# One loop per expert in the expert MLP, with tile numbers and the GELU table loaded once ahead of the loops

## The chip, the cores and the metric

The kernel runs on one core of a Trainium2 chip. The metric is the device time of one execution in microseconds (us). The kernel before takes 2174.18 us, the median of 3 runs (2167.58 to 2176.35).

## The reference, cut to what matters

The program is a graph block of two layers on 1250 nodes of 512 features. The change touches only the mixture of experts in the first layer: each token goes to 2 of 8 experts, and each expert is a two-layer MLP (512 to 2048 to 512 features) with an exact GELU. D is 512, E is 8 and K is 2.

```python
def _L0_ffn_ref(x, ln_g, ln_b, w_r, b_r, W1, b1, W2, b2):
    ...
    h = (x - mu) * jax.lax.rsqrt(var + LN_EPS) * ln_g + ln_b
    logits = jnp.einsum('btd,ed->bte', h, w_r) + b_r
    topk_vals, topk_idx = jax.lax.top_k(logits, K)
    gates = jax.nn.softmax(topk_vals, axis=-1)
    hf = h.reshape(B * T, d)
    hid = jax.nn.gelu(jnp.einsum('nd,edf->nef', hf, W1) + b1, approximate=False)
    expert_stack = jnp.einsum('nef,efd->ned', hid, W2) + b2
    ...
    return x + mixed
```

## The kernel before, in words

Every engine has its own program, written by hand; they meet at semaphores. Around 860 to 1500 us of the span stands the expert stage. Tokens have been sorted by expert into `tokens_sorted` and padded so that each tile of 128 rows belongs to one expert. `first_tile_int` holds nine whole numbers: `first_tile_int[e]` is the number of the first tile of expert e, and the last is the count of tiles. They come out of the data, so every engine reads them into registers to know where its loops end (`expert_bounds`, L719, one `value_load` per number, which is a TENSOR_LOAD at L721 and some register instructions).

On each of PE, ACT and DVE the stage is an outer loop of four rounds `i`, and in a round two inner loops over tiles `t`: `a = 0` for expert 2i, `a = 1` for expert 2i + 1 (even and odd expert below). Each engine reads three bounds at the start of a round. The weights lie in two sets of buffers, chosen by `a`: W1 and half of W2 in `big_a` or `big_b`, the other half in `wide`. SP loads them (L910 to L919): expert e + 2 as soon as the last tile of expert e is through.

A tile goes through 16 chunks `f` of 128 hidden units (`FC` = 16). PE multiplies W1's chunk with the transposed tile `tile_T` into one of four banks (L2571). ACT applies GELU with the expert's bias twice, into `hid` and rounded into `hid_hi` (L1370), and copies W2's chunk rounded into `w2_hi` (L1346). DVE takes the remainders, `hid_lo` (L1902) and `w2_lo` (L1909). Two chunks behind, PE multiplies three products of hidden and W2 parts into the bank of the result (L2561, L2562, L2563). Behind the last up-projection PE transposes the next tile's rows (L2541), and ACT and DVE each write half of `tile_T` (L1352, L1895); `down(14)` and `down(15)` follow on PE. DVE copies the result to `tile_out` (L1942). POOL has its own loop over all tiles, without experts: it loads the rows of the tile after next (L1117) when PE has transposed, and stores `tile_out` (L1120).

The text of ACT's inner loops does not load the table of GELU; the builder puts an ACT_TABLE_LOAD ahead of an activation wherever the table in place may be another. Before the stage it is the one of the square root (L1340). Whoever builds the first inner loop's body can't tell which table it finds, so that body holds two such loads.

Of the kernel before, what the change touches and what calls it, by code (L numbers as in the profile page):

```python
# [6 lines left out]
P = 128  # L7
# [37 lines left out]
def graph_block_kernel(nc, A, out):  # L45
# [5 lines left out]
    C = D // P  # L51
# [34 lines left out]
    with ctx:  # L86
# [1061 lines left out]
        def _(act):  # L1148
# [207 lines left out]
            act.wait_ge(tiles_ready, 1)  # L1356
            act.sem_inc(gelu_done, UP_BANKS)
            tile_T_half(1)
            with act.Fori(0, EX // 2) as i:
                bounds = expert_bounds(act, i)  # L1360
                for a in range(2):
                    lo, hi = bounds[a:a + 2]
                    with act.Fori(lo, hi) as t:
                        act.wait_ge(ew2_loaded[a], i * 32 + 32)
                        w2_leading(t, a, 0)
                        for f in range(FC):
                            act.wait_ge(up_done, t * FC + f + 1)
                            act.wait_ge(chunk_used, t * FC + f + 1)
                            for dst in (hid, hid_hi):
                                last = nc.scalar.activation(dst[:, f % HID_SLOTS, :], psum[:, f % UP_BANKS, 0:P], ACT.Gelu,  # L1370
                                                            bias=expert_bias_T[:, bass.ds(i * (2 * FC) + a * FC + f, 1)])
                            last.then_inc(gelu_done, 1)

                            if f + 1 < FC - 1:
                                w2_leading(t, a, f + 1)
                            if f == FC - 1:
                                w2_leading(t, a, f)
                        tile_T_half(t + 2)
# [171 lines left out]
        def _(dve):  # L1550
# [375 lines left out]
            dve.sem_inc(tile_out_ready, 1)  # L1926
            tile_transposed_out(1)
            dve.sem_inc(tile_out_free, 1)
            with dve.Fori(0, EX // 2) as i:
                bounds = expert_bounds(dve, i)  # L1930
                for a in range(2):
                    with dve.Fori(bounds[a], bounds[a + 1]) as t:
                        w2_rest(t, a, 0)
                        for f in range(FC):
                            hidden_rest(t, f)
                            if f + 1 < FC - 1:
                                w2_rest(t, a, f + 1)
                        w2_rest(t, a, FC - 1)
                        tile_transposed_out(t + 2)
                        dve.wait_ge(chunk_used, t * FC + FC + HID_SLOTS)  # L1940
                        dve.wait_ge(tile_out_free, t + 1)
                        nc.vector.tensor_copy(tile_out, psum[:, Y_BANK, :]).then_inc(tile_out_ready, 1)  # L1942
# [234 lines left out]
        def _(pe):  # L2177
# [357 lines left out]

            for b in range(8):
                pe.wait_ge(bank_free[b], before_experts[b])
# [9 lines left out]
            with pe.Fori(0, EX // 2) as i:  # L2547
                bounds = expert_bounds(pe, i)
                for a in range(2):
                    lo, hi = bounds[a:a + 2]  # L2550
                    pe.wait_ge(ew1_loaded[a], i * 32 + 32)
                    pe.sem_inc(loop_entered, 1)
                    with pe.Fori(lo, hi) as t:
                        def down(f):
                            if f == 0:
                                pe.wait_ge(tile_out_ready, t + 1)
# [227 lines left out]
```

## Time and profile before

| | us |
|---|---|
| median of 3 runs (lowest to highest) | 2174.18 (2167.58 to 2176.35) |
| the profiled execution's own time | 2170.96 |
| its span, from first to last instruction | 2169.3 |
| PE matmuls busy | 2046.8 (94%) |
| DVE busy | 1310.9 (60%) |
| ACT busy | 1056.2 (49%) |
| POOL busy | 527.6 (24%) |
| granted TensorE clock, mean | 0.974 of full speed |

A busy share is that of the whole span, of which the expert stage is some 630 us. "PE" are the matmuls, "PEld" the weight loads that overlap them; names ending in "q" are an engine's sequencer, whose register, branch and load instructions do not count as busy. "Issue" is idle time in which an engine waited for nothing that the profile shows. The granted clock of 1.0 is TensorE at 2.4 GHz, 0.5 at 1.2 GHz.

### The profile page before, as it was taken

How to read it: one execution, taken by the hardware profiler on the slowest of the kernel's cores; microseconds unless marked ns; L12 is line 12 of the kernel's file. 1: busy time of each engine (PE TensorE's matmuls, PEld its weight loads, DVE VectorE, ACT ScalarE, POOL GpSimd, SP SyncE). 2: the span in 40 equal slices, each digit the busy share in tenths (PEclk: the TensorE clock that was granted, in tenths of full speed). 3: DMA queues.
4: the chain of work that ended last, by engine and by line, in shares of the span. 5: the costliest groups of instructions: out<-in, count | busy, mean ns of one | idle time of the engine just before them, and what ended most of it. 6: DMA issues, size and time to landing. Idle time of an engine off the chain costs nothing.

```text
span 2169.3 us, 42548 instructions
## 1 busy us (share of the span) xinstructions
PE 2046.8 (94%) x13564; PEld 1485.4 (68%) x13565; DVE 1310.9 (60%) x2651; ACT 1056.2 (49%) x2327; POOL 527.6 (24%) x567
## 2 busy tenths in 40 slices
PE   7899899999999988999999999996899999999998
PEld 4544344444444466888888888885697888778886
DVE  3311699999999977555555555655613445644444
ACT  6531244444444422776777777774243322554443
POOL 3100477777766752100000000004000000400000
PEclk9999999999999997999999999998999999999999
DMA  6651588888888875548104400044500200310000
GB/s 217 227 175 45 157 238 238 239 237 236 238 238 238 237 302 189 207 174 298 51 19 174 174 19 19 19 174 158 194 11 10 88 20 20 112 44 10 10 10 19
DMA packets 141915, 297.44 MB, mean 137 GB/s; under 512 B 28925, under 2 KB 70662, under 8 KB 137239
## 3 DMA queue, kind: packets, MB, share of 16 engines
q1 hardware_dynamic: 96933, 159.09, 21.2%
q0 software_dynamic: 36592, 130.56, 19.9%
q10 hardware_dynamic: 8322, 6.89, 1.0%
q8 instruction: 43, 0.70, 0.1%
q14 instruction: 25, 0.20, 0.0%
HBM read 242.31 MB, written 54.17 MB: 137 GB/s over the span
## 4 chain that ended last, share of the span: by engine, by line
PE 86%; DVE 4%; issue 3%; ACT 3%; DMA 2%; POOL 1%; ACTq 0%; POOLq 0%; DVEq 0%; PEldq 0%
PE psum L2571 14%; PE psum L2425 11%; PE psum L2387 9%; PE psum L2710 7%; PE psum L2743 5%; PE psum L2616 4%; PE psum L2561 4%; PE psum L2562 4%; PE psum L2563 3%; PE psum L2607 3%; PE psum L2647 3%; PE psum L2413 3%; PE psum L2637 3%; PE psum L2286 2%; PE psum L2661 1%
## 5 line engine op out<-in xcount | busy, mean ns | idle before, releaser
L1068 POOL DMA_INDIRECT big_b<-sender_table,wide x360 | 376.8, 1047 | 209.4 <-issue 118.6
L2425 PEld LDWEIGHTS psum<-big_b,wide 128*32 128x32 f32 x3600 | 165.4, 109 | 193.5 <-issue 130.3
L2571 PEld LDWEIGHTS psum<-xn_T,big_b 128*128 128x128 f32 x2048 | 261.9, 191 | 21.2 <-issue 3.1
L1250 ACT ACTIVATE wide<-wide 128x290 bf16<-128x290 f32 x360 | 168.5, 527 | 219.8 <-PE psum L2425 161.9
L2425 PE MATMUL psum<-big_b,wide 128*32 128x256 f32 (+2 forms) x3600 | 270.0, 387 | 0.0
L2571 PE MATMUL psum<-xn_T,big_b 128*128 128x128 f32 x2048 | 265.0, 275 | 0.0
L2387 PE MATMUL psum<-w_mlp,wide 64*128 64x512 f32 x728 | 206.2, 643 | 5.3 <-DVE big_b L1733 3.6
L1909 DVE TENSOR_TENSOR w_lo<-wide,w_hi 128x512 fp32r<-128x512 f32 x184 | 127.3, 692 | 117.9 <-ACT w_hi L1346 117.9
L2561 PE MATMUL psum<-w_hi,hid_hi 128*128 128x512 f32 x368 | 176.1, 478 | 10.1 <-DVE w_lo L1909 7.2
L1733 DVE TENSOR_TENSOR big_b<-big_b,psum 128x768 f32<-128x768 f32 x180 | 169.4, 941 | 0.0
L1732 DVE TENSOR_TENSOR big_b<-big_b,psum 128x768 f32<-128x768 f32 x180 | 168.7, 937 | 0.0
L2710 PE MATMUL psum<-xn_T,wide 128*128 128x256 f32 (+1 forms) x640 | 154.7, 388 | 2.9 <-ACT shid_hi L1542 2.9
L1346 ACT ACTIVATE w_hi<-wide 128x512 fp32r<-128x512 f32 x184 | 115.8, 629 | 70.7 <-PE psum L2563 70.7
L2562 PE MATMUL psum<-w_hi,hid_lo 128*128 128x512 f32 x368 | 146.1, 397 | 0.0
L2563 PE MATMUL psum<-w_lo,hid_hi 128*128 128x512 f32 x368 | 144.3, 392 | 0.0
L1370 ACT ACTIVATE xn_T<-psum,table 128x128 f32<-128x128 f32 x368 | 130.6, 355 | 25.4 <-PE psum L2571 25.3
L1117 POOL DMA_DIRECT2D xn_T<-tokens_sorted x23 | 12.5, 542 | 527.3 <-PE psum L2541 527.3
L2710 PEld LDWEIGHTS psum<-xn_T,wide 128*128 128x128 f32 (+1 forms) x640 | 123.9, 195 | 23.4 <-issue 3.9
L2571 PEld LDWEIGHTS psum<-xn_T,big_a 128*128 128x128 f32 x896 | 121.9, 202 | 20.5 <-issue 12.6
L1370 ACT ACTIVATE hid_hi<-psum,table 128x128 fp32r<-128x128 f32 x368 | 133.7, 363 | 0.0
L2571 PE MATMUL psum<-xn_T,big_a 128*128 128x128 f32 x896 | 123.8, 287 | 10.3 <-issue 10.3
L1909 DVE TENSOR_TENSOR w_lo<-big_b,w_hi 128x512 fp32r<-128x512 f32 x128 | 88.4, 691 | 74.6 <-ACT w_hi L1346 74.6
(457 smaller groups left out, 3680.9 us busy)
## 6 DMA issues: line engine op xcount, KB each, us to landing
big_a<-in_L_ffn_W SPq DMA_DIRECT2D x12, 2048.0 KB, 13.8
big_b<-in_L_ffn_W SPq DMA_DIRECT2D x12, 2048.0 KB, 13.4
wide<-in_L_ffn_W SPq DMA_DIRECT2D x8, 2048.0 KB, 23.5
wide<-edge_hidden SPq DMA_DIRECT2D x91, 128.0 KB
edge_hidden<-wide SPq DMA_DIRECT2D x21, 512.0 KB, 3.0
tokens_sorted<-zeros SPq DMA_DIRECT2D x29, 256.0 KB, 3.4
adj_dram<-big_a SPq DMA_DIRECT2D x1, 6400.0 KB, 23.3
xn_T<-tokens_sorted POOLq DMA_DIRECT2D x25, 256.0 KB, 2.9
```

Of the source, the lines that this page charges most:

```text
L1068: nc.gpsimd.indirect_dma_start(out=sent[q][:, j, :], out_offset=None, in_=sender_table, in_offset=bass.IndirectOffsetOnAxis(ap=record[k][q ...
L1370: last = nc.scalar.activation(dst[:, f % HID_SLOTS, :], psum[:, f % UP_BANKS, 0:P], ACT.Gelu, bias=expert_bias_T[:, bass.ds(i * (2 * FC) + ...
L1732: nc.vector.tensor_tensor(prod[q][:, :, 5:8, :], s1, w[:, :, 2:3, :].to_broadcast([P, 2, 3, MUL]), ALU.mult)
L1733: nc.vector.tensor_tensor(prod[q][:, :, 2:5, :], s1, w[:, :, 3:4, :].to_broadcast([P, 2, 3, MUL]), ALU.mult)\
L1909: nc.vector.tensor_tensor(w2_lo[:, f % 2, :], w2, w2_hi[:, f % 2, :].bitcast(F32), ALU.subtract).then_inc(w2_split, 1)
L2387: last = nc.tensor.matmul(tile_w[q % 2][:, j, :], h3_slot[q][halves[j], :], w_mlp4[halves[j], :], start=True, stop=True)
L2425: return nc.tensor.matmul(msg_psum[k].rearrange("p (c u) -> p c u", u=MUL)[bands[g], cols, :], hot_y[q][:, j, y, :], p[:, of, :], start=Fa ...
L2561: nc.tensor.matmul(psum[:, Y_BANK, :], hid_hi[:, h, :], w2_hi[:, w, :], start=(f == 0), stop=False)
L2562: nc.tensor.matmul(psum[:, Y_BANK, :], hid_lo[:, h, :], w2_hi[:, w, :], start=False, stop=False)
L2563: nc.tensor.matmul(psum[:, Y_BANK, :], hid_hi[:, h, :], w2_lo[:, w, :], start=False, stop=(f == FC - 1))\
L2571: last = nc.tensor.matmul(psum[:, f % UP_BANKS, 0:P], ew1[a][:, c, f * P:f * P + P], tile_T[:, c, :], start=(c == 0), stop=(c == C - 1))
L2710: last = nc.tensor.matmul(out_b[0:r, 0:n], sw1_cols[:, c, j * P:j * P + r], xn_T[:, c, n0:n0 + n], start=(c == 0), stop=(c == C - 1))
```

## The change

The outer loop over pairs is unrolled: on PE, ACT and DVE there are now eight loops over tiles, one per expert. The bounds of all experts are read once, ahead of them (eight reads per engine; expert 0 starts at 0), at a place where `tiles_ready` says that they are there. ACT loads the GELU table once, by hand, behind its reads and ahead of the first `tile_T` half. The wait for W2's weights stands once per expert ahead of ACT's loop. The bias of a chunk is addressed by a constant. PE no longer reads the count of tiles behind the loops. SP and POOL are unchanged.

```diff
-        def expert_bounds(eng, i):
-
-            return [eng.value_load(first_tile_int[0:1, bass.ds(2 * i + k, 1)], min_val=min(k, 1), max_val=TILES - (k < 2))
-                    for k in range(3)]
+        def expert_bounds(eng):
+
+            return [0] + [eng.value_load(first_tile_int[0:1, e:e + 1], min_val=e, max_val=TILES - (EX - e)) for e in range(1, EX + 1)]
...
             act.wait_ge(tiles_ready, 1)
+            bounds = expert_bounds(act)
+            nc.scalar.preload_act_table(ACT.Gelu)
             act.sem_inc(gelu_done, UP_BANKS)
             tile_T_half(1)
-            with act.Fori(0, EX // 2) as i:
-                bounds = expert_bounds(act, i)
-                for a in range(2):
-                    lo, hi = bounds[a:a + 2]
-                    with act.Fori(lo, hi) as t:
-                        act.wait_ge(ew2_loaded[a], i * 32 + 32)
-                        w2_leading(t, a, 0)
...
-                                                            bias=expert_bias_T[:, bass.ds(i * (2 * FC) + a * FC + f, 1)])
...
+            for e in range(EX):
+                a = e % 2
+                act.wait_ge(ew2_loaded[a], e // 2 * 32 + 32)
+                with act.Fori(bounds[e], bounds[e + 1]) as t:
+                    w2_leading(t, a, 0)
...
+                                                        bias=expert_bias_T[:, e * FC + f:e * FC + f + 1])
...
             dve.sem_inc(tile_out_ready, 1)
+            dve.wait_ge(tiles_ready, 1)
+            bounds = expert_bounds(dve)
             tile_transposed_out(1)
             dve.sem_inc(tile_out_free, 1)
-            with dve.Fori(0, EX // 2) as i:
-                bounds = expert_bounds(dve, i)
-                for a in range(2):
-                    with dve.Fori(bounds[a], bounds[a + 1]) as t:
...
+            for e in range(EX):
+                a = e % 2
+                with dve.Fori(bounds[e], bounds[e + 1]) as t:
...
             transposes(("biasT",), [bias_rows[:, :]])
 
+            pe.wait_ge(tiles_ready, 1)
+            bounds = expert_bounds(pe)
             for b in range(8):
                 pe.wait_ge(bank_free[b], before_experts[b])
 
...
             pe.wait_ge(tile_loaded, 16)
             tile_transposes()
             pe.sem_inc(chunk_used, HID_SLOTS)
-            with pe.Fori(0, EX // 2) as i:
-                bounds = expert_bounds(pe, i)
-                for a in range(2):
-                    lo, hi = bounds[a:a + 2]
-                    pe.wait_ge(ew1_loaded[a], i * 32 + 32)
-                    pe.sem_inc(loop_entered, 1)
-                    with pe.Fori(lo, hi) as t:
...
-            count = pe.value_load(first_tile_int[0:1, EX:EX + 1], min_val=EX, max_val=TILES)
-            pe.wait_ge(tile_out_ready, count + 1)
-            pe.wait_ge(tile_T_ready, count + 1)
-            pe.wait_ge(tile_T_half_ready, count + 1)
+            for e in range(EX):
+                a = e % 2
+                pe.wait_ge(ew1_loaded[a], e // 2 * 32 + 32)
+                with pe.Fori(bounds[e], bounds[e + 1]) as t:
...
+            pe.wait_ge(tile_out_ready, bounds[EX] + 1)
+            pe.wait_ge(tile_T_ready, bounds[EX] + 1)
+            pe.wait_ge(tile_T_half_ready, bounds[EX] + 1)
```

How the instructions stand, at two places. First ACT, where it enters the stage and the first even expert's loop. Before (L1352 is the first `tile_T` half, L1346 the copy of W2's chunk into `w2_hi`, L1370 the GELU; "table" in a TENSOR_LOAD is the buffer that holds the tile numbers):

```order
L1352 ACTIVATE xn_T<-psum,table 128x128 x2
L1359 UNCONDITIONAL_BRANCH
L1359 ISA
L721 TENSOR_LOAD table
L721 ISA x3
...
L1363 UNCONDITIONAL_BRANCH
L1363 ISA
L1345 ISA
L1346 ACT_TABLE_LOAD
L1346 ACTIVATE w_hi<-big_a 128x512
...
L1370 ACT_TABLE_LOAD
L1370 ACTIVATE xn_T<-psum,table 128x128
```

And of the change (the line numbers are one less):

```order
L721 TENSOR_LOAD table
L721 ISA x2
...
L1357 ACT_TABLE_LOAD
L1351 ACTIVATE xn_T<-psum,table 128x128 x2
L1363 UNCONDITIONAL_BRANCH
L1363 ISA
L1345 ACTIVATE w_hi<-big_a 128x512
L1366 REGISTER_ALU
L1369 ACTIVATE xn_T<-psum,table 128x128
L1369 ACTIVATE hid_hi<-psum,table 128x128
```

The reads, eight now, and one table load have moved ahead of the first `tile_T` half; the two table loads inside the loop are gone, and the register instruction ahead of each GELU pair with them. The next ACT_TABLE_LOAD stands behind the last expert's loop (L1300).

Second PE, where the stage begins and at the end of a round. Before (L2541 are the four transposes, L2553 is the loop over tiles, L2547 the one over pairs):

```order
L2541 MATMUL psum<-ident,xn_T 128x128 x4
L2547 UNCONDITIONAL_BRANCH
L2547 ISA
L721 TENSOR_LOAD table
L721 ISA x3
...
L2571 MATMUL psum<-xn_T,big_a 128x128 x4
...
L2553 COMPARE_AND_BRANCH
L2547 REGISTER_ALU
L2547 COMPARE_AND_BRANCH
L2580 TENSOR_LOAD table
```

And of the change, at the start of the stage and from the loop of one expert to that of the next (L2543 are the transposes, L2552 is the loop over tiles):

```order
L721 TENSOR_LOAD table
L721 ISA x2
L2543 MATMUL psum<-ident,xn_T 128x128 x4
L2552 UNCONDITIONAL_BRANCH
...
L2552 COMPARE_AND_BRANCH
L2552 UNCONDITIONAL_BRANCH
L2552 ISA
L2568 ISA
L2570 MATMUL psum<-xn_T,big_b 128x128 x4
```

The reads stand ahead of the wait for the first tile, not between the transposes and the first up-projection, and between two experts there are only the end of one loop and the start of the next.

## Rows read from the trace of the kernel before

**Rows 1.** The page, chain that ended last: shares of the span by line.

```profile
PE psum L2571 14%; PE psum L2425 11%; PE psum L2387 9%; PE psum L2710 7%; PE psum L2743 5%; PE psum L2616 4%; PE psum L2561 4%; PE psum L2562 4%; PE psum L2563 3%; PE psum L2607 3%; PE psum L2647 3%; PE psum L2413 3%; PE psum L2637 3%; PE psum L2286 2%; PE psum L2661 1%
```

**Rows 2.** Timeline of POOL: start, length (us), engine, line, operation.

```profile
897.10 0.56 POOL L1117 DMA_DIRECT2D xn_T<-tokens_sorted  x1 [18.17 <-PE psum L2541]
...
1496.76 0.61 POOL L1117 DMA_DIRECT2D xn_T<-tokens_sorted  x1 [5.27 <-PE psum L2541]
```

**Rows 3.** Stretches between L1117's issues: engines' busy us (count), PEclk, DMA share, GB/s.

```profile
897.10:924.54 27.44, 26.42 (x180) 23.64 (x180) 15.79 (x36) 21.54 (x53) 1.11 (x3) 1.00 0.22 83
951.00:977.43 26.43, 26.12 (x180) 23.57 (x180) 15.71 (x36) 18.87 (x51) 1.08 (x3) 1.00 0.06 21
977.43:1009.49 32.06, 29.09 (x180) 26.23 (x180) 15.80 (x36) 21.54 (x53) 1.08 (x3) 0.89 0.75 278
1141.69:1171.93 30.24, 26.61 (x180) 23.64 (x180) 15.79 (x36) 21.54 (x53) 1.08 (x2) 1.00 0.79 295
...
1410.83:1442.89 32.06, 29.14 (x180) 26.29 (x180) 15.81 (x36) 21.55 (x53) 1.09 (x3) 0.89 0.75 278
```

**Rows 4.** The same of PE, from a tile's first up-projection to L1117's issue.

```profile
1010.51:1035.95 25.44, 25.36 (x178) 1.00 0.95 350
1145.49:1171.93 26.44, 25.64 (x177) 1.00 0.82 321
...
981.28:1009.49 28.21, 28.12 (x177) 0.90 0.78 301
869.08:897.10 28.02, 27.90 (x177) 0.91 0.81 308
```

**Rows 5.** ACT's table loads in the stage: busy us, mean ns | idle before.

```profile
L1346 ACT ACT_TABLE_LOAD x7 | 9.0, 1283 | 6.9 <-issue 6.8
L1370 ACT ACT_TABLE_LOAD x7 | 9.0, 1283 | 6.3 <-PE psum L2571 6.1
```

**Rows 6.** Timeline at expert 4's entry; in brackets idle time before, and releaser.

```profile
1145.49 2.94 PE L2571 MATMUL psum<-xn_T,big_a 128*128 128x128 f32 x24 [2.61 <-issue]
...
1146.75 1.28 ACT L1370 ACT_TABLE_LOAD   x1 [1.35 <-PE psum L2571]
...
1149.14 0.47 PE L2561 MATMUL psum<-w_hi,hid_hi 128*128 128x512 f32 x1 [0.72 <-DVE hid_lo L1902]
```

**Rows 7.** Line 721 at that entry, by sequencer: ns min/median/max, first and last start.

```profile
L721 ACTq TENSOR_LOAD <-table x3: 273/275/281, 1141.5 to 1142.7; - x3
...
L721 PEldq TENSOR_LOAD <-table x3: 298/301/307, 1142.6 to 1144.2; - x3
...
L721 DVEq TENSOR_LOAD <-table x3: 300/300/314, 1143.7 to 1145.1; - x3
```

**Rows 8.** Waits of the expert stage: us in total, times, longest.

```profile
ACT w_hi L1346 <- PE psum L2563: 137.9, 299, 1.3
```

**Rows 9.** Timeline of PE at the start of the stage.

```profile
865.57 1.08 PE L2541 MATMUL psum<-ident,xn_T 128*128 128x128 f32 x4 [7.59 <-DMA xn_T<-tokens_sorted]
869.08 5.45 PE L2571 MATMUL psum<-xn_T,big_a 128*128 128x128 f32 x24 [2.42 <-issue]
```

**Rows 10.** Timelines of DVE and of ACT at the same place.

```profile
866.69 0.73 DVE L1895 TENSOR_SCALAR xn_T<-psum,table 128x128 f32<-128x128 f32 x2 [7.25 <-PE psum L2541]
...
866.69 0.81 ACT L1352 ACTIVATE xn_T<-psum,table 128x128 f32<-128x128 f32 x2 [8.49 <-PE psum L2541]
```

**Rows 11.** Expert 3's last weights: issue in SP's timeline, and line 919's landing.

```profile
980.41 10.18 SPq L919 DMA_DIRECT2D wide<-in_L_ffn_W  x1
...
DMA to landing us min/median/max: 23.9/23.9/23.9
```

**Rows 12.** Timeline of DVE in the first tile of expert 3.

```profile
1011.41 0.68 DVE L1909 TENSOR_TENSOR w_lo<-big_b,w_hi 128x512 fp32r<-128x512 f32 x1
```

**Rows 13.** DMA queues between 850 and 1120 us: packets, MB, share.

```profile
q8 instruction: 4, 0.07, 0.1%
```

More of the change, by code:

```diff
@@ L1926, in _ @@
             dve.sem_inc(tile_out_ready, 1)
+            dve.wait_ge(tiles_ready, 1)
+            bounds = expert_bounds(dve)
             tile_transposed_out(1)
             dve.sem_inc(tile_out_free, 1)
[L1929 to L1942 removed]
+            for e in range(EX):
+                a = e % 2
+                with dve.Fori(bounds[e], bounds[e + 1]) as t:
+                    w2_rest(t, a, 0)
+                    for f in range(FC):
+                        hidden_rest(t, f)
+                        if f + 1 < FC - 1:
+                            w2_rest(t, a, f + 1)
+                    w2_rest(t, a, FC - 1)
+                    tile_transposed_out(t + 2)
+                    dve.wait_ge(chunk_used, t * FC + FC + HID_SLOTS)
+                    dve.wait_ge(tile_out_free, t + 1)
+                    nc.vector.tensor_copy(tile_out, psum[:, Y_BANK, :]).then_inc(tile_out_ready, 1)
             for t in range(NT + 1):
@@ L2580, in _, with down @@
-            count = pe.value_load(first_tile_int[0:1, EX:EX + 1], min_val=EX, max_val=TILES)
-            pe.wait_ge(tile_out_ready, count + 1)
-            pe.wait_ge(tile_T_ready, count + 1)
-            pe.wait_ge(tile_T_half_ready, count + 1)
+            for e in range(EX):
+                a = e % 2
+                pe.wait_ge(ew1_loaded[a], e // 2 * 32 + 32)
+                with pe.Fori(bounds[e], bounds[e + 1]) as t:
+                    def down(f):
+                        if f == 0:
+                            pe.wait_ge(tile_out_ready, t + 1)
+                        pe.wait_ge(w2_split, t * FC + f + 1)
+                        pe.wait_ge(hid_split, t * FC + f + 1)
+                        h, w = f % HID_SLOTS, f % 2
+                        nc.tensor.matmul(psum[:, Y_BANK, :], hid_hi[:, h, :], w2_hi[:, w, :], start=(f == 0), stop=False)
+                        nc.tensor.matmul(psum[:, Y_BANK, :], hid_lo[:, h, :], w2_hi[:, w, :], start=False, stop=False)
+                        nc.tensor.matmul(psum[:, Y_BANK, :], hid_hi[:, h, :], w2_lo[:, w, :], start=False, stop=(f == FC - 1))\
+                            .then_inc(chunk_used, 1)
+                    pe.wait_ge(tile_T_ready, t + 1)
+                    pe.wait_ge(tile_T_half_ready, t + 1)
+                    for f in range(FC):
+                        pe.wait_ge(gelu_done, t * FC + f + 1)
+                        for c in range(C):
+                            last = nc.tensor.matmul(psum[:, f % UP_BANKS, 0:P], ew1[a][:, c, f * P:f * P + P], tile_T[:, c, :],
+                                                    start=(c == 0), stop=(c == C - 1))
+                        last.then_inc(up_done, 1)
+                        if f >= 2:
+                            down(f - 2)
+                    pe.wait_ge(tile_loaded, t * 16 + 32)
+                    tile_transposes()
+                    down(FC - 2)
+                    down(FC - 1)
```

46 lines of the change are left out of this document (11 added, 35 removed).

## The prediction

> **What bounds the kernel now.** I read the page first: its chain of waits gives the expert stage's matmuls (L2571, L2561 to L2563) 25% of the span [rows 1]. Such a share does not say what an edit of that stage is worth, so I went to the stage itself. POOL reloads `tile_rows` once per tile (L1117), always behind the same four transposes on PE, so its issues are a clock with one tick per tile. There are 23 ticks, the first at 897.10 us and the last at 1496.76 [rows 2]: 599.66 us for 22 periods, 27.26 us each. The table of stretches between two ticks [rows 3] shows that they are not alike. A tile of an odd expert takes 26.43 us, the second tile of expert 0 takes 27.44, and the first tile of experts 2, 4 and 6, behind the turn of the pair loop, takes 32.06, 30.24 and 32.06. From the ticks, experts 0 to 7 have 2, 2, 1, 5, 2, 8, 2 and 1 tiles. PE is 26.12 us busy in the 26.43 of a plain tile, and ACT waits for PE in nearly every chunk (137.9 us over 299 waits, 0.46 us each [rows 8]). So PE bounds a plain tile, and what only relieves ACT or a sequencer inside it can't show; what can move is the excess over some 26.44 us.
>
> **What makes up the excess.** The next table measures from the first up-projection of a tile to the next tick [rows 4]: 25.44 us in an odd tile; 26.44 in the first tile of expert 4, at full clock; 28.21 in that of expert 2, where the granted clock averages 0.90 (part of the stretch stands at the lower level, 1.2 GHz); 28.02 at 0.91 in the first tile of all. So at full clock the body of an even tile costs 1.00 us more than an odd one. The order of instructions names what the even body has and the odd one has not: two ACT_TABLE_LOADs per tile, in seven tiles, 1283 ns each [rows 5]. That is 2.57 us of ACT, of which 1.00 reaches PE: the rest lies beside PE's 24 up-projection matmuls, which run ahead of the first GELU. The timeline of expert 4's entry [rows 6] shows both parts: PE waits 2.61 us ("issue") before the up-projection at 1145.49, and 0.72 us more at 1149.14 for hid_lo, which is late behind the second table load at 1146.75. In the first of these gaps the sequencers make three TENSOR_LOADs each, of 0.30 us and with register work behind them, so that on PE their starts lie 0.8 us apart, on DVE 0.7 and on ACT 0.6 [rows 7].
>
> **The change, part by part.**
> - *Table loads out of the even tiles.* All eight loops now hold Copy, Gelu and Identity alone, and one load stands ahead of them. Six even tiles at 1.00: **6.0 us** (the seventh, the stage's first tile, is counted below).
> - *Tile numbers no longer read at a pair's start.* Of expert 4's 30.24 us, 26.44 are a plain tile and 1.00 the tables, so its entry is 2.80; three entries: **8.4 us**. What an entry costs afterwards is what the step from an even to an odd expert costs now: expert 1's first period runs from 924.54 to 951.00, 26.46 [rows 3], 0.02 over a plain one. At 0.04 for each of seven entries, **0.3 us** is given back.
> - *Clock.* Experts 2 and 6 take 1.82 us longer than expert 4 with the same work, at a granted clock of 0.89 against 1.00 [rows 3], and the lower level comes after PE's 2.6 us pause. Without the pause I take the dip as gone: **3.6 us**. Ends: 0, if both dips stay, and 3.6.
> - *First tile.* PE starts its last four transposes at 865.57 and the up-projection only at 869.08 [rows 9], since all three engines first enter the pair loop and read its bounds. Now only `tile_T` is needed; ACT's half of it takes 0.81 us from 866.69 [rows 10], so the start can be near 867.7, 1.4 us earlier. But PE stands at the lower level here (24 matmuls in 5.45 us, against 2.94 at full clock [rows 6]), and time won at half speed is worth half if the clock rises when it did. Ends 0.7 and 1.4; I take **1.0**. The tables cost nothing in this tile, since 28.02 less 25.44 is 2.58 and the slow matmuls alone account for 2.51 of it.
> - *Eight reads ahead of the stage, per engine.* By the spacing above, 6.4 us on PE, 5.6 on DVE, 4.8 on ACT. Their cover is the wait for the first tile's rows: PE is idle for 7.59 us up to 865.57 [rows 9], DVE for 7.25 and ACT for 8.49 up to 866.69 [rows 10]. ACT has the table load, 1.28, on top. All is hidden, by 1.2 us at the least. If a read cost a third of a whole entry, 0.93, eight would be 7.5: PE just in time, DVE 0.2 late, ACT (8.7 in all) 0.3 late. I take 0, with 0.3 as the other end.
> - *Register work off ACT.* The bias address needs no register any more, and ACT waits on `ew2_loaded` once per expert, not per tile: 0, because ACT waits for PE in the chunks [rows 8]. PE's read behind the loops goes too: 0, as PE waits there for the first z rows anyway.
> - *Which transfer comes next?* Only expert 3's weights have a single tile (expert 2's) to arrive in. Their last part is issued at 980.41 and lands 23.9 us later, at 1004.3 [rows 11], 26.9 us after the tick at 977.43. Now expert 2's tile ends 26.44 after it, and ACT wants that weight at once: some 0.4 us late. But DVE takes its remainder only at 1011.41 [rows 12], 1.92 behind the tick at 1009.49, and the copy before it takes 0.6, so up to about 1.3 us is swallowed. 0, with 1 us as the bad end.
>
> **Sum.** 6.0 + 8.4 - 0.3 + 3.6 + 1.0 = 18.7 us. From the other side: 22 periods of 26.44 are 581.7, against 599.66 now; the 17.9 between them answer to the 17.7 of the terms without the first tile. The profiled execution took 2170.96 us, so it would become 2152.3. It lies 3.2 us below the median of the runs shown, 2174.18 (2167.58 to 2176.35); against that median, on which I forecast, it is **2155.5 us**.
>
> **A rule weighed.** Entries by the outer loop's back branch idle PE 2.61 us [rows 6], and the very first entry, which no back branch precedes, 2.42 [rows 9]: the jump back over two bodies costs 0.2 us at most, and a back branch over one body or the first run through expert 1's code costs nothing that the period shows (26.43 and 26.46) [rows 3]. "Runtime: NRT & Kernel Launch" of the Trainium skill, section Instruction fetch mechanics, says that a taken branch stalls for a fetch when its target is outside a small window of recent pages. By it the back branch could be most of the 8.4 us, which leaves the sum as it is; but it also speaks against this change, which makes four times the loop code. What that would do here is rival 2.
>
> **The rivals.**
> 1. *The gap stays.* If PE's pause is loop set-up and not the reads, every even entry keeps it and only the tables and the first tile's end go: 6.0 + 1.0 = 7.0 us, 2167.2. For it: the view says "issue". Against: three reads at 0.8 fill 2.4 of the 2.6 us, and odd experts enter the same kind of loop without a gap. 5%.
> 2. *The code of eight bodies does not stay at hand* (slower). A tile's body is 180 matmuls and 180 weight loads on PE, with waits between [rows 3], and the instruction queue brought in only 4 pieces between 850 and 1120 us [rows 13]: once through experts 0 and 1, then looped. If now the branch back inside each expert had to fetch its body anew, each of 15 such branches (23 tiles, 8 experts) could cost as much as the entry gap, 2.61 us: 39.2 us, less 18.7, or 2194.7. The point from which it decides is 18.7 / 15 = 1.25 us per branch. Against it: one body is half of the pair that stayed at hand, and each loop is as long as before. 4%.
> 3. *The clock keeps its dips*, due by time and not to the pause. For it: expert 4's entry has the pause and no dip. Against: two of three pauses have one, and long stretches without a pause have none. 18.7 - 3.6 = 15.1, 2159.1. 13%.
> 4. *The loads stay where they were.* In the changed order no table load stands in the loops and no TENSOR_LOAD between them, so this is 1%, at 2174.
>
> **Numbers.** Forecast 77%; rivals 5, 4, 13 and 1%. About 0.5%, 10.9 us, is what a measurement of this kernel can tell from no change. The range takes the sum's ends (a gain of 14.8 to 19.1), rival 3, and a median that may fall some 4 us to either side as the runs shown do: 2147 to 2164; rivals 1, 2 and 4 stay outside. Faster: forecast and rival 3 less 2% for their slow edge, 0.88. Same: that edge and rivals 1 and 4, 0.08. Slower: rival 2, 0.04.
>
> **What would show it.** One ACT_TABLE_LOAD at L1357 near 863 us and none in the tiles; ticks of POOL's reload 26.4 apart from first to last, so some 582 us in all; PE's "issue" idle before the up-projection under 1 us per entry; eight TENSOR_LOADs per engine, done before 866; a granted clock of 1.00 from the second tile to the last. It is wrong if ticks within an expert grow, if the first tick comes later than 897, or if what the stage saves returns behind it, in the wait for the z rows.

## The result, and the profile after

The changed kernel takes 2155.49 us (median of 6 runs, 2150.12 to 2160.32), the kernel before 2171.59 in 6 runs beside it (2167.58 to 2176.35). The ratio is 0.9918, with a 95% interval of 0.9902 to 0.9934: faster by 0.8%. The profiled execution took 2152.54 us, 18.4 less than the 2170.96 of before; the prediction's sum was 18.7. By the medians the gain is 16.1.

| | before | after |
|---|---|---|
| profiled execution / its span, us | 2170.96 / 2169.3 | 2152.54 / 2151.0 |
| PE, DVE busy, us | 2046.8, 1310.9 | 2038.7, 1311.0 |
| ACT, POOL busy, us | 1056.2, 527.6 | 1037.8, 545.9 |
| first and last tick of POOL's reload | 897.10, 1496.76 | 896.10, 1477.66 |
| 22 periods | 599.66 | 581.56 |
| last tick to the end of the span | 672.5 | 673.3 |

So 18.1 us came from the 22 periods, the first tick stands 1.0 earlier, and 0.8 went again behind the stage: 18.3 of span. The ticks, in POOL's timeline of the changed kernel (start, length, line; they answer to [rows 2]):

```profile
896.10 0.56 POOL L1116 DMA_DIRECT2D xn_T<-tokens_sorted  x1 [17.42 <-PE psum L2543]
...
1477.66 0.61 POOL L1116 DMA_DIRECT2D xn_T<-tokens_sorted  x1 [5.28 <-PE psum L2543]
```

The stretches between ticks, of the changed kernel (length, then busy us of PE, PEld, DVE, ACT and POOL with counts, granted clock, DMA share, GB/s). In order: second tile of expert 0, expert 1's first, experts 2's and 4's first, and the stage's last but one. They answer to [rows 3]:

```profile
896.10:922.53 26.43, 26.13 (x180) 23.58 (x180) 15.71 (x36) 18.84 (x51) 1.11 (x2) 1.00 0.26 96
922.53:948.94 26.41, 26.12 (x180) 23.58 (x180) 15.69 (x36) 18.81 (x51) 1.09 (x2) 1.00 0.90 338
975.38:1001.81 26.43, 26.12 (x180) 23.58 (x180) 15.71 (x36) 18.82 (x51) 1.08 (x2) 1.00 0.90 338
1133.98:1160.42 26.44, 26.12 (x180) 23.58 (x180) 15.72 (x36) 18.84 (x51) 1.08 (x3) 1.00 0.90 338
1424.78:1451.22 26.44, 26.12 (x180) 23.57 (x180) 15.72 (x36) 18.83 (x51) 1.09 (x3) 1.00 0.06 20
```

Every one of the 22 periods lies between 26.41 and 26.47. The 27.44 of the even tile is gone (ACT has 51 instructions there instead of 53 and 2.7 us less busy time), and so are the 32.06, 30.24 and 32.06 of the entries. PE is busy 26.12 of 26.44 in all of them; the clock is 1.00 throughout. At expert 4's entry, where before stood 2.61 of issue [rows 6], PE's timeline now shows only the wait that every tile has:

```profile
1134.21 0.50 PE L2560 MATMUL psum<-w_hi,hid_hi 128*128 128x512 f32 x1 [0.32 <-DVE w_lo L1908]
1134.55 0.40 PE L2561 MATMUL psum<-w_hi,hid_lo 128*128 128x512 f32 x1
1134.78 0.39 PE L2562 MATMUL psum<-w_lo,hid_hi 128*128 128x512 f32 x1
1135.01 2.74 PE L2570 MATMUL psum<-xn_T,big_a 128*128 128x128 f32 x23
```

The waits of the 22 periods (total, times, longest) say what bounds a tile now. PE waits for one thing alone, the last w_lo of a tile, 0.3 us each time:

```profile
...
DVE w_lo L1908 <- ACT w_hi L1345: 217.9, 331, 1.1
ACT w_hi L1345 <- PE psum L2562: 134.7, 286, 0.8
...
PE psum L2560 <- DVE w_lo L1908: 6.9, 22, 0.3
```

The start of the stage is the one place that does not look as forecast. PE's timeline there (it answers to [rows 9]):

```profile
860.69 0.24 PE L2446 MATMUL psum<-ident,src_int 24*128 24x24 f32 x1
865.17 1.09 PE L2543 MATMUL psum<-ident,xn_T 128*128 128x128 f32 x4 [4.24 <-DMA xn_T<-tokens_sorted]
```

ACT's timeline at the same place, against [rows 10], and then line 721 by sequencer (ns min/median/max, first and last start):

```profile
860.97 0.19 ACT L1341 ACTIVATE table<-psum 128x24 f32<-128x24 f32 x1 [15.49 <-PE psum L2446]
866.02 1.28 ACT L1357 ACT_TABLE_LOAD   x1 [4.86 <-issue]
867.31 0.81 ACT L1351 ACTIVATE xn_T<-psum,table 128x128 f32<-128x128 f32 x2
```

```profile
L721 PEldq TENSOR_LOAD <-table x8: 296/335/563, 855.0 to 860.1; - x8
...
L721 ACTq TENSOR_LOAD <-table x8: 273/280/553, 861.0 to 864.9; - x8
L721 DVEq TENSOR_LOAD <-table x8: 297/314/582, 861.1 to 865.7; - x8
```

The transposes end at 866.26, but ACT is not through with its eight reads and the table load before 867.30, so its half of tile_T starts 1.0 us late, and PE's first up-projection behind a wait of 2.10 for it. ACT began its reads late because PE's work ahead of L2446 ended late: the same 20 matmuls of L2532 took 14.19 us before, at a granted clock of 0.62, and take 17.43 now, at 0.50, which is the lower level of 1.2 GHz. PE's timelines, before and after:

```profile
843.75 14.19 PE L2532 MATMUL psum<-w_mlp,xn_T 8*128 8x512 f32 x20
```

```profile
843.47 17.43 PE L2532 MATMUL psum<-w_mlp,xn_T 8*128 8x512 f32 x20
```

### The profile page after: what moved, and what is told of

It reads as the page before. It is cut to its first block, busy times and chain, and to the rows that moved or that the text cites. A ratio compares the mean times of both kernels' runs of the same rounds, so it can differ in the third digit from the quotient of the medians.

```text
span 2151.0 us, 42029 instructions
## 1 busy us (share of the span) xinstructions
PE 2038.7 (95%) x13564; PEld 1480.0 (69%) x13565; DVE 1311.0 (61%) x2651; ACT 1037.8 (48%) x2314; POOL 545.9 (25%) x567
## 4 chain that ended last, share of the span: by engine, by line
PE 87%; DVE 4%; ACT 3%; issue 2%; DMA 2%; POOL 1%; ACTq 0%; POOLq 0%; DVEq 0%; PEldq 0%
PE psum L2570 14%; PE psum L2425 12%; PE psum L2387 9%; PE psum L2708 7%; PE psum L2741 5%; PE psum L2614 4%; PE psum L2560 4%; PE psum L2561 4%; PE psum L2562 3%; PE psum L2605 3%; PE psum L2413 3%; PE psum L2645 3%; PE psum L2635 3%; PE psum L2286 2%; PE psum L2659 1%
## 5 line engine op out<-in xcount | busy, mean ns | idle before, releaser
L1067 POOL DMA_INDIRECT big_b<-sender_table,wide x360 | 395.3, 1098 | 191.1 <-issue 79.4
L1730 DVE TENSOR_TENSOR big_b<-psum,big_b 128x512 f32<-128x512 f32 x180 | 121.2, 673 | 9.6 <-DMA big_b<-sender_table,wide 9.5
L2570 PEld LDWEIGHTS psum<-xn_T,big_a 128*128 128x128 f32 x896 | 116.9, 195 | 11.5 <-issue 3.6
```

Source lines behind the costliest of these rows:

```text
L1067: nc.gpsimd.indirect_dma_start(out=sent[q][:, j, :], out_offset=None, in_=sender_table, in_offset=bass.IndirectOffsetOnAxis(ap=record[k][q ...
L2570: last = nc.tensor.matmul(psum[:, f % UP_BANKS, 0:P], ew1[a][:, c, f * P:f * P + P], tile_T[:, c, :], start=(c == 0), stop=(c == C - 1))
```

## The experiments

Kernels of one group ran on one chip, beside the kernel before. The two kernels with added table loads in the first group, and all in the second, the kernel before among them, have one run each. In the first two groups the kernel before took 2243.15 and 2251.33 us; the work ahead of the stage is some 70 us longer there (first tick at 968.55 in the first run below, 897.10 in [rows 2]). Why is not known; the first and the third group bear the same chip number, so the chip does not explain it. So I read the stage by its ticks; the periods of plain tiles are the same there, 26.43 to 26.48. A period is named by the tile that it ends in.

### Which part of the gain is whose (first group)

**Table load alone ahead of the pair loop**, in the kernel before:

```diff
+            nc.scalar.preload_act_table(ACT.Gelu)
             act.sem_inc(gelu_done, UP_BANKS)
             tile_T_half(1)
```

> The kernel before, with one GELU table load by hand ahead of the first tile_T half; the pair loop and its reads stay, and the 14 table loads in the tiles vanish. My theory (a pair of loads in an even tile costs PE 1.00 us, the rest is covered): the second tiles of experts 0, 4 and 6 fall from 27.4 to 26.44 us, the first tiles of experts 2, 4 and 6 from 32.06, 30.24 and 32.06 to about 31.06, 29.24 and 31.06; first to last reload of tile_rows from 599.66 to about 593.7 us; the kernel 6 us faster. Rival (every load counts in full, 2.57 us a tile): second tiles 24.9 us or the stage some 15 us shorter. Rival (the loads carry the entry's gap too): entries fall to 26.44.

Measured: 2236.42 us, ratio 0.9971 (0.9956 to 0.9986). The stretches of expert 0's second tile, and of the entries of experts 2, 4 and 6:

```profile
968.55:995.02 26.47, 26.17 (x180) 23.56 (x180) 15.70 (x36) 18.86 (x51) 1.11 (x2) 1.00 0.12 41
1047.92:1078.89 30.97, 27.99 (x180) 25.20 (x180) 15.90 (x36) 19.09 (x51) 1.09 (x3) 0.94 0.77 288
1211.10:1240.39 29.29, 26.36 (x180) 23.57 (x180) 15.81 (x36) 18.99 (x51) 1.08 (x3) 1.00 0.81 304
1478.33:1509.24 30.91, 28.00 (x180) 25.20 (x180) 15.89 (x36) 19.09 (x51) 1.08 (x2) 0.94 0.77 288
```

Expert 0's second tile fell from 27.44 to 26.47, and experts 4's and 6's likewise (26.43, 26.44): 1.0 us per even tile, as the first term has it. One call ahead of the loops is enough; the builder puts no load into the loops then. Expert 4's entry keeps 29.29 less 26.44, 2.85 us, with PE's 2.61 of issue; two of three entries keep their dip, 1.6 to 1.7 us.

**The reads back at a pair's start, everything else as changed.** Eight loops stay, one table load stays ahead, and each engine reads three bounds by constant address ahead of each even expert's loop:

```diff
+                if a == 0:
+                    bounds = pair_bounds(pe, e)
-                with pe.Fori(bounds[e], bounds[e + 1]) as t:
+                with pe.Fori(bounds[a], bounds[a + 1]) as t:
```

> The changed kernel, with three tile numbers read on PE, ACT and DVE at the start of every even expert's loop, where the pair loop read them, and none ahead of the stage. Eight loops and the one table load stay. My theory (the entry's gap is the reads): first tiles of experts 2, 4 and 6 take about 29.2 us at full clock, or 31.0 where the granted clock falls after the pause; the stage from first to last reload 581.6 + 8.4 = 590.0, plus 1.8 for each dip; the kernel 8 to 14 us slower than the changed one. Rival (the gap is the pair loop's own branch or set-up): these tiles stay at 26.4 to 26.7 us and the time does not move.

Measured: 2230.42 us, ratio 0.9944 (0.9923 to 0.9964). The entries of experts 2, 4 and 6, and PE at expert 4's:

```profile
1053.73:1082.00 28.27, 26.37 (x180) 23.57 (x180) 15.80 (x36) 18.94 (x51) 1.08 (x2) 1.00 0.84 317
1214.18:1242.49 28.31, 26.36 (x180) 23.57 (x180) 15.80 (x36) 18.96 (x51) 1.08 (x3) 1.00 0.85 316
1480.40:1508.70 28.30, 26.37 (x180) 23.57 (x180) 15.80 (x36) 18.94 (x51) 1.08 (x2) 1.00 0.84 316
```

```profile
1217.00 1.27 PE L2580 MATMUL psum<-xn_T,big_a 128*128 128x128 f32 x9 [1.63 <-issue]
```

An entry costs 1.87 us over 26.43, not the 2.80 that the kernel before paid. The reads by constant address start 0.65 us apart on PE:

```profile
L725 PEldq TENSOR_LOAD <-table x3: 296/298/302, 1214.7 to 1216.0; - x3
```

Before it was 0.80 [rows 7], and there one more register instruction stood behind each. So of the 2.85 of an entry at full clock, two thirds are three reads as such; the other 0.98 is the address worked out from `i` and the turn of the outer loop, which this run does not tell apart. An estimate from the spacings: 0.15 more for each of three reads is 0.45, and some 0.5 is left for the turn of the loop. None of the three entries has a dip.

**Where a table load hides.** With the eight loops as changed, one more load per tile at the loop's start, and then loads on either side of the first copy:

```diff
                 with act.Fori(bounds[e], bounds[e + 1]) as t:
+                    if True:
+                        nc.scalar.preload_act_table(ACT.Gelu)
                     w2_leading(t, a, 0)
```

> The changed kernel, with one more GELU table load at the start of each of the 23 tiles, ahead of the copy of W2's first chunk. My theory (ACT waits 1.48 us for the first up-projection there, which covers 1.28): a tile stays at 26.44 us, the stage at 581.6. Rival (a load goes on the path in full, 1.28 each): 27.7 a tile, the stage 28 us longer.

> The changed kernel, with three more GELU table loads in each of the 23 tiles: one ahead of the copy of W2's first chunk and two behind it, ahead of the first GELU. My theory (a fixed cover of about 1.9 us at a tile's start, from 1.48 us of ACT's wait and some 0.4 us until hid_lo of chunk 0 is late for PE): 3.85 - 1.9 = 1.9 to 2.0 us a tile, so 28.4 us a tile and the stage about 43 us longer. Rival (no cover, 3.85 a tile): 30.3 a tile, 85 us longer. Rival (chunks catch up, since ACT has slack in each chunk): 26.44.

Measured with one: 2220.06 us, and no tile is longer, though ACT is 1.4 us busier:

```profile
1201.85:1228.28 26.43, 26.12 (x180) 23.57 (x180) 15.78 (x36) 20.23 (x52) 1.08 (x2) 1.00 0.91 338
```

In the second kernel the builder dropped one of the two loads that stood in a row, so it has two per tile, not three (x22 each in ACT's groups, 1283 ns), and it measures what two cost: 27.27 to 27.29 in every tile but the last, +0.84 for 2.57 us of ACT. PE waits once more than in a plain tile, at the first down-projection; the rest of the 0.84 is its busy time, 26.36 against 26.12 for the same matmuls:

```profile
1218.91:1246.20 27.29, 26.36 (x180) 23.65 (x180) 15.80 (x36) 21.52 (x53) 1.08 (x2) 1.00 0.86 328
```

```profile
1223.41 0.47 PE L2564 MATMUL psum<-w_hi,hid_hi 128*128 128x512 f32 x1 [0.61 <-DVE hid_lo L1905]
```

The cover is thus between 1.28 and 2.57, and 1.73 if all that passes it counts in full. Two loads cost 0.84 here and 1.00 in the even tiles of before. They stand at other places: before, the second one began only behind the wait for the up-projection [rows 6], here it stands ahead of that wait. That this is the 0.16 between them is not shown; that the 1.00 belongs to the loads is shown by the run with the table load alone. The last tile took 36.66 here, and 29.36 in the run with the table load alone; see the end of this section.

### Whose reads cost, and when the clock falls (second group)

**Reads back on PE alone, on ACT and DVE alone, and six reads instead of three on all.** The edits are that of the reads above, on the engines named; for six, `for n in (e, e + 1, e + 2, e, e + 1, e + 2)`.

> The changed kernel with the three reads at the start of each even expert on PE alone; ACT and DVE keep theirs ahead of the stage. With all three engines reading there, an entry takes 28.3 us, 1.87 more than a plain tile. My theory (PE's own reads are the gap, 1.63 us of them idle, since the other engines' start earlier or have cover): 28.1 to 28.3 us for the first tiles of experts 2, 4 and 6. Rival (DVE, last to read, sets the end): about 26.6 to 27.0. Rival (reads of the engines add up): near 27.1.

> The changed kernel with the three reads at the start of each even expert on ACT and DVE, and PE's ahead of the stage. My theory (ACT's copy of W2's first chunk comes 1.0 us late, which its wait covers; DVE's reads end some 1.2 to 1.4 us behind where w_lo of chunk 0 would start, which PE feels by 0 to 0.6 us): 26.4 to 27.1 us for the first tiles of experts 2, 4 and 6. Rival (DVE sets the end): 28.3.

> reads_back with every number read twice: six reads per engine at the start of an even expert. My theory (0.65 us per read with a constant address, on PE's path): an entry of 28.3 + 1.95 = 30.2 us at full clock. For the clock: if it falls because PE stood still long enough (it did in two of three pauses of 2.6 us and in none of 1.6 us), it falls behind at least two of these pauses of 3.6 us, and those entries take about 32. Rival (the dips were due to something else in the pair loop): 1.00 throughout and 30.2 for all three.

| reads at an even entry | time | entries 2, 4, 6 | over 26.44 | PE's issue idle | dips |
|---|---|---|---|---|---|
| three on all | 2230.42 | 28.27, 28.31, 28.30 | 1.85 | 1.63 | 0 of 3 |
| three on PE | 2239.72 | 28.44, 28.29, 28.31 | 1.9 | 1.62 | 0 of 3 |
| three on ACT and DVE | 2233.38 | 27.37, 27.36, 27.36 | 0.92 | none; 0.69 for hid_lo | 0 of 3 |
| six on all | 2248.52 | 31.87, 31.84, 31.87 | 5.4 | 3.54 | 3 of 3 |

The first row is the kernel of the first group. PE's own reads set the entry; the same reads on ACT and DVE come to rest behind them when all three read, and alone they still cost half, as hid_lo comes late. The last row's stretch, with the clock at 0.95, and PE at expert 4's entry:

```profile
1220.11:1251.95 31.84, 27.99 (x180) 25.20 (x180) 15.89 (x36) 19.09 (x51) 1.08 (x3) 0.95 0.75 281
```

```profile
1224.83 1.65 PE L2580 MATMUL psum<-xn_T,big_a 128*128 128x128 f32 x8 [3.54 <-issue]
```

PE's busy time tells the dip apart from the pause: 27.99 against 26.36 for the same 180 matmuls, 1.63 us. So three more reads added 1.9 of pause and 1.6 of clock. Over all runs, pauses of 1.6 us brought no dip (0 of 6), of 2.6 us two in three (the same two in the kernel before and in the one with the table load alone), of 3.5 us three in three. The dips belong to the pauses; why expert 4's entry escapes at 2.6 us is not shown.

**Three table loads per tile, kept apart** so that the builder drops none:

```diff
+                    nc.scalar.preload_act_table(ACT.Gelu)
                     w2_leading(t, a, 0)
+                    nc.scalar.preload_act_table(ACT.Gelu)
...
                         last.then_inc(gelu_done, 1)
+                        if f == 0:
+                            nc.scalar.preload_act_table(ACT.Gelu)
```

> The changed kernel with three table loads per tile and an activation between each, so that the builder keeps all three (of the two in a row in three_loads_all it kept one, and that run had two per tile: 27.28 us, 0.84 over a plain tile for 2.57 of loads, a cover of 1.73): ahead of W2's first copy, behind it, and behind the first chunk's GELU pair. My theory (one cover for the start of a tile, 1.73 us, and what passes it goes to PE in full): 3.85 - 1.73 = 2.1 us over, 28.5 to 28.6 us per tile. Rival (ACT's slack of 0.44 us in each chunk takes up a load placed behind the first chunk): 27.3 to 27.7.

Measured: 2268.21 us, 28.23 per tile, +1.79 for 3.85 us of ACT where 2.1 was expected. The third load, behind the first GELU, is late at the second down-projection and costs 0.95 of its 1.28:

```profile
1233.35 0.47 PE L2564 MATMUL psum<-w_hi,hid_hi 128*128 128x512 f32 x1 [0.61 <-DVE hid_lo L1905]
1235.89 0.47 PE L2564 MATMUL psum<-w_hi,hid_hi 128*128 128x512 f32 x1 [0.72 <-DVE hid_lo L1905]
```

The cover at a tile's start is used up by the first two, and only 0.33 of the third is taken up elsewhere.

### Can the start and the tile's end be had too? (third group)

Beside 11 runs of the kernel before (2171.84 us, 2168.36 to 2177.25), the changed kernel again, one with ACT's reads and table load ahead of its copy of the biases (a copy that waits for PE), and one with two more edits at a tile's end. There DVE wrote its half of tile_T ahead of the last w_lo, and PE waited for w_lo only ahead of the third product:

```diff
             nc.scalar.activation(dinv[:, :], full[:, 0:NT], ACT.Sqrt).then_inc(free, 1)
+            nc.scalar.preload_act_table(ACT.Gelu)
+            act.wait_ge(tiles_ready, 1)
+            bounds = expert_bounds(act)
             full, free = filled(act, ("biasT",))
...
-            act.wait_ge(tiles_ready, 1)
-            bounds = expert_bounds(act)
-            nc.scalar.preload_act_table(ACT.Gelu)
             act.sem_inc(gelu_done, UP_BANKS)
```

```diff
-                        pe.wait_ge(w2_split, t * FC + f + 1)
+                        pe.wait_ge(w2_hi_ready, t * FC + f + 1)
...
+                        pe.wait_ge(w2_split, t * FC + f + 1)
                         nc.tensor.matmul(psum[:, Y_BANK, :], hid_hi[:, h, :], w2_lo[:, w, :], start=False, stop=(f == FC - 1))\
```

> The changed kernel itself, beside the next two on the same chip. 22 tile periods of 26.44 us, 581.6 from first to last reload of tile_rows; against the kernel before a ratio near 0.992, or 0.9917 if the 18 us of the stage are all of it.

> The changed kernel with ACT's table load and its eight reads moved further ahead, before the wait for biasT's transpose, where ACT is idle. My theory (ACT's reads and the load end 0.9 us behind the first transposes now and hold up the first half of tile_T): the time from the first transposes on PE to the first reload of tile_rows falls from 30.9 us to 30.1 to 30.5, all other periods stay; the whole 0.4 to 0.9 us, too little to be seen in the time. Rival (DVE's reads end as late as ACT's and bind next): 30.9 again.

> early, and in each tile two more edits: PE waits for w2_lo only ahead of the third product of a chunk (for w2_hi ahead of the first), and DVE writes its half of the next tile_T ahead of the last chunk's w2_lo. My theory (a plain tile is 16 chunks of 1.587 us = 25.39 and 1.05 at its end, of which PE waits 0.3 for w2_lo and the next up-projection another 0.2 behind tile_T): 26.15 to 26.25 us per tile, the stage near 576, the kernel about 5 us faster than early. Rival (the end of a tile is bound by the chain over ACT's and DVE's tile_T halves alone, so PE's earlier matmuls only wait elsewhere): 26.44.

| | time (lowest to highest) | ratio | 22 periods | first transposes to first tick |
|---|---|---|---|---|
| changed, again | 2156.45 (2153.75 to 2162.22) | 0.9930 (0.9915 to 0.9946) | 581.64 | 31.05 |
| early reads | 2154.84 (2149.33 to 2158.45) | 0.9912 (0.9897 to 0.9927) | 581.57 | 29.15 |
| early reads, both edits | 2165.79 (2159.83 to 2167.15) | 0.9963 (0.9949 to 0.9978) | 589.20 | 30.23 |

The early reads do what they should at their place. PE's timelines at the start, of the changed kernel run again and then of the early one:

```profile
874.05 5.40 PE L2570 MATMUL psum<-xn_T,big_a 128*128 128x128 f32 x24 [2.00 <-ACT xn_T L1351]
```

```profile
875.89 4.41 PE L2570 MATMUL psum<-xn_T,big_a 128*128 128x128 f32 x24 [1.09 <-DVE xn_T L1894]
```

The wait falls by 0.91. Another 0.99 is the clock, granted at 0.65 over the early kernel's first 24 matmuls and at 0.52 over the other's. The second part is not the edit's doing: the two kernels below have the same early reads, their 24 matmuls took 5.48 at 0.51 and 0.50, and from first transposes to first tick they took 30.23 and 30.38. In the whole time the two kernels can't be told apart: 1.6 us between medians, within overlapping intervals.

The kernel with both edits is slower than that by 11 us, where a gain was expected: its periods are 26.71 to 26.89, which makes 7.6 of the 11. PE's and DVE's timeline at a tile's end shows two late things:

```profile
1169.90 0.73 DVE L1894 TENSOR_SCALAR xn_T<-psum,table 128x128 f32<-128x128 f32 x2
...
1170.55 0.68 DVE L1908 TENSOR_TENSOR w_lo<-wide,w_hi 128x512 fp32r<-128x512 f32 x1
...
1171.28 0.50 PE L2563 MATMUL psum<-w_lo,hid_hi 128*128 128x512 f32 x1 [0.25 <-DVE w_lo L1908]
...
1171.92 2.75 PEld L2571 LDWEIGHTS psum<-xn_T,big_a 128*128 128x128 f32 x24 [0.46 <-issue]
```

The last w_lo is ready some 0.4 us later, and only one product lies between it and the next tile. One more kernel parts the two edits: DVE's order as it was, PE's wait split.

> The kernel with the early reads, and of the two edits of the one before only TensorE's: it waits for w_hi ahead of the first product of a down-projection chunk and for w_lo ahead of the third; VectorE keeps its order (last w_lo, then its half of tile_T). In the kernel with both edits a tile took 26.78 us where 26.43 was expected to shrink: VectorE's half of tile_T pushed the last w_lo from 1.55 to 1.97 us after the start of the transposes, and after the third product 0.46 us of issue idle stood ahead of the next tile's first weight load, 0.19 before. Theory A (VectorE's order is what cost, TensorE's wait alone is a gain): w_lo is there 1.55 us after the transposes' start, before the second product ends, the idle 0.31 goes, and the next bound is VectorE's half of tile_T, done 2.2 us after the transposes' start where the up-projection now begins at 2.41: a tile of 26.25 to 26.35 us, 22 tiles 2 to 4 us less than with the early reads alone, ratio to the kernel before 0.990 to 0.991. Theory B (the turn of TensorE's loop, end and entry waits, was hidden under three queued products and no longer is): the idle ahead of the first weight load grows by what the wait gives back, and a tile stays at 26.43 or grows up to 26.6, ratio 0.991 to 0.994.

Measured: 2152.93 us (2149.32 to 2153.51) beside 9 runs of the kernel before, 2170.75 (2167.91 to 2176.21), ratio 0.9908 (0.9891 to 0.9924); periods of 26.41 to 26.47, 581.59 in all. So DVE's order, beside the split wait, is what cost 0.35 us per tile, and PE's split wait alone is worth nothing. DVE's order was not tried without the split wait. Why nothing, at one tile's end:

```profile
1162.45 0.72 DVE L1894 TENSOR_SCALAR xn_T<-psum,table 128x128 f32<-128x128 f32 x2
...
1162.59 0.49 PE L2563 MATMUL psum<-w_lo,hid_hi 128*128 128x512 f32 x1
...
1163.30 2.75 PEld L2571 LDWEIGHTS psum<-xn_T,big_a 128*128 128x128 f32 x24 [0.53 <-issue]
1163.31 2.94 PE L2571 MATMUL psum<-xn_T,big_a 128*128 128x128 f32 x24 [0.22 <-DVE xn_T L1894]
```

PE's pause has moved behind the third product. The transposes began at 1160.98, w_lo was there 1.55 us after that and DVE's half of tile_T 2.19 after, both as theory A has them, and the up-projection begins at 2.33 instead of 2.41. The 0.08 is given back at once: the weight loads no longer run ahead there, so the 24 matmuls take 2.94 us and not 2.86. The profile also puts 0.53 down to issue ahead of the weight load, as theory B had it; which of the two would last longer without the other is not tried. The stage is at the same pace by either.

**Open.** In the first two groups the stage's last tile, beside which POOL issues ten indirect gathers, took 29.36, 36.66, 31.40, 31.07, 29.70 and 31.52 us in six of eight kernels, 26.44 or 26.45 in the other two (one table load per tile, three reads on all), and 26.44 after the change here. It stands in kernels with and without table loads and reads, so none of the edits explains it, and I left it out of the readings; its cause was not tried.

## Why the prediction was right, and where its terms were off

Forecast: 2155.5 us, faster. Measured: 2155.49. That the two agree to 0.01 is luck. The gain was forecast at 18.7 against a median of 2174.18 from three runs; over six runs that median is 2171.59, and the gain by medians is 16.1 (15.4 when the changed kernel ran again). The base and the gain each came out 2.6 us lower, and that cancels. The mechanism is better judged by the profiled executions, 18.4 against 18.7, and by the ticks. The sum's ends are not all in the "gain of 14.8 to 19.1": 14.8 leaves out the 0.3 of the reads and the 1 us of expert 3's weights, with which the low end is 13.5. By its terms:

- **Table loads, 6.0.** Right. Expert 0's second tile fell by 1.01, and with the load alone moved the even second tiles fell by 0.94 to 0.97. The reason given, cover beside the 24 up-projection matmuls, holds in kind: one load per tile costs 0.00, two 0.84.
- **Pair entries, 8.4.** The size is right (2.80 forecast, 2.85 in the run with only the table load moved). What it is made of is not all as put: "three reads at 0.8 fill 2.4 of the 2.6 us" charged all register work to the read, but three reads by constant address cost 1.87, and about 0.98 goes with the dynamic address and the outer loop. So some 0.5 us per entry (the estimate above) is the loop set-up that rival 1 took for the whole pause. The change removed both.
- **New entries, −0.3.** Mis-sized: 0. All seven entries show 26.41 to 26.44, like a plain tile. This is most of the 0.4 by which the stage did better, 18.1 against 17.7.
- **Clock, 3.6.** Right, and rival 3 falls: no period after is below 1.00, and the runs tie the dips to the pause's length.
- **First tile, 1.0.** The first tick is 1.0 earlier, but that is partly luck. The rows land 0.4 earlier (transposes at 865.17 against 865.57), and from transposes to tick the gain is only 31.53 less 30.93, 0.6, under the lower end of 0.7. Of it 0.31 is the start (3.20 behind the transposes' start, 3.51 before, where 1.4 was forecast) and 0.29 the 24 matmuls, 5.16 against 5.45, at a granted clock of 0.55 against 0.51. With the reads out of the way the start comes 2.17 behind the transposes, 1.34 earlier than before, as forecast, and in the kernel whose clock stayed at 0.50 there (the last one tried) the gain to the tick was 1.15, 31.53 less 30.38. So the term fell short because the next one failed.
- **Eight reads ahead, 0.** This is the step that failed. It took ACT's cover as the 8.49 us of idle [rows 10]; but that idle begins behind ACT's copy of the biases, which waits for PE (L2446), and PE's last work ahead of the stage ended 3 us later in this execution (860.69, 857.74 before), while the rows landed no later. The cover was 5.1 us, from 861.16 to the end of the transposes at 866.26, and reads with table load took 6.1: 1.0 late. With them put ahead of that copy PE's wait went from 2.00 to 1.09. The table load at 866.02, not "near 863", is the same miss. PE's 3 us are the clock of the 20 matmuls ahead (0.62 before, 0.50 after), and not this change's doing: of the 14 traces 11 have 17.43 us there, while the kernel before, the one with the table load alone and the one with three loads kept apart have 14.05 to 14.19. That last one has ACT's reads and load where the changed kernel has them, its idle stretch was long, and they cost nothing: the load ended at 937.83, ahead of transposes that began at 938.62. Its PE timeline:

```profile
916.91 14.06 PE L2536 MATMUL psum<-w_mlp,xn_T 8*128 8x512 f32 x20
...
940.79 4.72 PE L2574 MATMUL psum<-xn_T,big_a 128*128 128x128 f32 x24 [1.09 <-issue]
```

  So the step read the cover off one execution and took it as fixed. What decides whether the clock rises in those 20 matmuls is not shown.
- **Expert 3's weights, 0 with 1 as the bad end.** Right: 0.85 late, forecast 0.4, and swallowed, since that period is 26.43. ACT's timeline in expert 3's first tile:

```profile
1002.80 0.63 ACT L1345 ACTIVATE w_hi<-big_b 128x512 fp32r<-128x512 f32 x1 [0.85 <-DMA wide<-in_L_ffn_W]
1003.95 0.37 ACT L1369 ACTIVATE xn_T<-psum,table 128x128 f32<-128x128 f32 x1 [0.51 <-PE psum L2570]
```

- **Rival 2, code not at hand.** Not so at this size. The instruction queue brought 7 pieces between 850 and 1120 us instead of 4 [rows 13], 53 in the whole span instead of 43, and no tick grew:

```profile
q8 instruction: 7, 0.11, 0.2%
```

  Neither the first run through a body nor the jump back over one costs anything that a period shows. The Trainium skill, "Runtime: NRT & Kernel Launch", section Instruction fetch mechanics, says that a taken branch stalls for a fetch when its target is outside the current window of pages. No stall of that kind is seen here in 22 periods of 26.41 to 26.47 us.
- **Behind the stage.** 0.8 us was lost there in the profiled execution. In the three traces of the third group and that of the last kernel the same stretch is 672.1 to 673.2 long, so 0.8 is within what it varies by.

## What to carry to other kernels

Find a clock inside a loop (here one DMA issue per tile) and list every period of it: four lengths that came back in a pattern gave all four terms. An idle stretch covers added work only from the moment at which the added work itself may start, so look at what stands ahead of it in that engine's own program. It is also only as long as the other engines leave it in that execution: here it was 3 us shorter where TensorE's granted clock had stayed at 0.50. Move reads of constants and table loads ahead of the last wait that can be late. A tensor engine's pause costs twice where it is long enough for the clock to fall behind it.

## What the runs showed of the hardware that I had not expected

- A `value_load` by constant address holds PE up by 0.65 us (0.73 each for the eight ahead of the stage), ACT by 0.56 (eight from 861.0 to 864.9) and DVE by 0.66, while the TENSOR_LOAD itself takes 0.28 to 0.34 in the median (at the longest 0.58); by a dynamic address 0.80 on PE.
- A pause of PE of 1.6 us left the clock at 1.00 in all entries, one of 2.6 did so in one of three only, one of 3.5 in none. A dip cost 1.6 us of matmul time by the runs (27.99 against 26.36 busy), and 1.8 us of period in the kernel before.
- The same 20 matmuls ahead of the stage took 14.05 to 14.19 us in 3 traces and 17.43 in the other 11, at a granted clock of 0.62 and of 0.50 where it was read.
- The builder drops a second table load in a row, and a load by hand ahead of a loop keeps it from putting its own into the loop.
- An order on DVE that serves the later consumer first (tile_T ahead of w_lo) cost 0.35 us per tile (beside PE's split wait) although DVE is only 60% busy: both results stand in one chain between the transposes and the next tile.
